# One expert ahead in the feed-forward stage: software pipelining of the two matmul phases on eight cores

## The reference

```python
probs = softmax(xf @ router_w + router_b)          # 64 experts
tw, ti = top_k(probs, 8); tw = tw / sum(tw)
...
def body(acc, p):                                  # p: one of 64 experts, hidden width 256
    W1, B1, W2, B2, e = p
    h = silu(xf @ W1 + B1) @ W2 + B2
    cw = sum(where(ti == e, tw, 0.0), axis=-1)
    return acc + cw[:, None] * h
...
shared = sum over 2 experts, hidden width 2048, of silu(xf @ SW1 + SB1) @ SW2 + SB2
```

## Time and profile before

| | |
|---|---|
| median of 2 runs | 8694.64 us (8684.18 to 8705.1) |
| the profiled execution | 8689.07 us |
| its span on the slowest core (core 5) | 8687.5 us |
| spans of cores 0 to 3 | 8566.1 to 8582.3 us |
| spans of cores 4 to 7 | 8629.4 to 8687.5 us |
| feed-forward stage from its first routed unit | about 4150 to 8500 us |

### The profile page before, as it was taken

The page is one execution under the profiler, slowest core; times in us unless marked ns, Lnnn a source line. Parts: engine busy times, 40 slices in busy tenths (PEclk is TensorE's granted clock), DMA queues, the critical chain, the costliest instruction groups (busy, mean ns, idle before and its releaser), DMA issues.

```text
span 8687.5 us, 72076 instructions; the slowest of 8 cores (8566.1 to 8687.5 us)
## 1 busy us (share of the span) xinstructions
PE 5028.5 (58%) x21600; PEld 2213.4 (25%) x21600; DVE 2143.5 (25%) x4862; ACT 1571.8 (18%) x3527; POOL 246.9 (3%) x300
## 2 busy tenths in 40 slices
PE   3554544645454545421666666666666667668881
PEld 1221221222222222210222222222222222223440
DVE  2333333331323222234111111111111111111113
ACT  1222222121212121222111111111111111111112
POOL 0000000001010000000000000000000000000000
PEclk8666666767575756655788887888888887777885
DMA  2000000005030312110211111111111001111202
GB/s 49 10 20 10 10 20 10 10 10 70 8 45 11 40 19 34 22 31 19 37 20 20 20 20 20 20 20 20 20 20 20 9 11 20 20 20 20 39 1 75
DMA packets 265490, 200.20 MB, mean 23 GB/s; under 512 B 142020, under 2 KB 224068, under 8 KB 265110
## 3 DMA queue, kind: packets, MB, share of 16 engines
q0 software_dynamic: 244448, 128.23, 11.4%
q1 hardware_dynamic: 20662, 67.36, 2.2%
HBM read 307.00 MB, written 16.78 MB: 37 GB/s over the span
## 4 chain that ended last, share of the span: by engine, by line
PE 54%; DVE 16%; ACT 13%; issue 11%; DMA 4%; DVEq 1%; ACTq 1%; another core or an unknown queue 1%; POOL 0%; POOLq 0%; SPq 0%
PE pb L158 54%; DVE h_sc L1046 3%; ACT h_sb L1039 2%; DVE S_state L555 2%; ACT cwb_sb L1021 2%; DVE st_sq L365 2%; DVE st_s L359 2%; DMA wog_buf<-Wog 2%; DVE khb L536 1%; ACT khT L547 1%; ACT xln_fm L406 1%; DVEq L80 1%; DVE st_s L1049 1%; DMA wk_buf<-Wk 1%; ACT Sbf L750 1%
## 5 line engine op out<-in xcount | busy, mean ns | idle before, releaser
L158 PE MATMUL pb<-w2g,h_sc 128*128 128x512 bf16 x5120 | 1678.9, 495 | 881.2 <-DVE st_s L1049 797.2
L158 PE MATMUL pb<-x1ln_fm,w1g 128*128 128x384 bf16 (+1 forms) x7680 | 1339.6, 336 | 283.7 <-ACT cwb_sb L1021 283.7
L158 PEld LDWEIGHTS pb<-w2g,h_sc 128*128 128x128 bf16 x5120 | 575.9, 118 | 1862.6 <-issue 1723.2
L158 PEld LDWEIGHTS pb<-x1ln_fm,w1g 128*128 128x128 bf16 x7680 | 745.9, 107 | 831.6 <-issue 442.4
L1046 DVE TENSOR_TENSOR h_sc<-h_sb,cwb_sb 128x384 bf16<-128x384 bf16 (+1 forms) x768 | 257.9, 336 | 2812.8 <-ACT h_sb L1039 2770.1
L1076 DVE TENSOR_TENSOR acc<-acc,pb 128x512 f32<-128x512 f32 x640 | 439.8, 687 | 736.5 <-PE pb L158 685.2
L1039 ACT ACTIVATE h_sb<-pb,b1T_sb 128x384 bf16<-128x384 f32 (+1 forms) x768 | 419.2, 546 | 955.4 <-PE pb L158 953.8
L1021 ACT CAST cwb_sb<-pb 128x384 bf16<-128x384 f32 (+1 forms) x384 | 170.3, 444 | 2201.5 <-PE pb L158 2201.5
L158 PE MATMUL pb<-Wv_sb,xln_fm 128*128 128x512 bf16 x2048 | 445.1, 379 | 0.0
L158 PE MATMUL pb<-v_tm,khT 128*128 128x256 bf16 x512 | 189.8, 371 | 288.8 <-ACT khT L547 216.9
L158 PE MATMUL pb<-iI128b,khb 128*128 128x128 bf16 x512 | 141.9, 277 | 335.7 <-DVE khb L536 335.7
(11 more groups left out here) (146 smaller groups left out, 3805.0 us busy)
## 6 DMA issues: line engine op xcount, KB each, us to landing
w1g<-w POOLq DMA_DIRECT2D x64, 512.0 KB, 14.1
w2g<-w POOLq DMA_DIRECT2D x64, 512.0 KB, 15.7
x_tm<-x_pre SPq DMA_DIRECT2D x12, 2048.0 KB, 9.2
wog_buf<-Wog POOLq DMA_DIRECT2D x64, 256.0 KB, 4.6
x_tm<-x_own SPq DMA_DIRECT2D x4, 2048.0 KB, 7.6
wq_buf<-Wq POOLq DMA_DIRECT2D x32, 256.0 KB, 5.1
wk_buf<-Wk POOLq DMA_DIRECT2D x32, 256.0 KB, 5.2
x_sp<-x_tm SPq DMA_DIRECT2D x16, 512.0 KB, 2.6
```

Source lines behind the costliest of these rows:

```text
L158: fn = lambda E, o=out, l=lhsT, r=rhs, st=start, sp=stop: E.matmul(o, l, r, start=st, stop=sp)
```

## The change

The loop body over the four units of a tile is cut in two functions. `front` holds everything up to the product with `cwb_sb`, `back` the 12 (or 4) matmuls with `w2g`. `back` of a unit is now emitted after `front` of the next one, and the last `back` of a tile after the one before it. `cwb_sb` and `h_sc` get two places, used in turn (`par`); `h_sb` is gone, the `Silu` writes `h_sc` and the product is formed in place. All three matmul groups of a front go into one bank, `pb[6 + par]`. The copy on `st_s1` is gone; TensorE waits for the product itself. The first ScalarE write of a front waits for the product of the front two before (`scale_tok`).

```diff
-                for j, (kind, e) in enumerate(grp):
+                def front(j, kind, e):
+                    par = j % 2
+                    bankh = pb[6 + par]
                     b.wait("t", wtoks[slot])
                     if kind == "r":
-                        bank6 = pb[6]
                         b.wait("t", tk_cwT)
-                        mm(b, bank6, bank6.sl(0, tscnt),
+                        mm(b, bankh, bankh.sl(0, tscnt),
                            selg[:, j * 128:(j + 1) * 128],
                            cwT64[:, ts0:ts0 + tscnt], start=True, stop=True, seal=True)
...
+                        b.wait("s", scale_tok[par])
+                        pbread(b, bankh, "s",
+                               lambda E, bankh=bankh, par=par, tscnt=tscnt: E.copy(
+                                   cwb_sb[:, par, 0:tscnt], bankh.sl(0, tscnt)))
+                    else:
+                        b.wait("s", scale_tok[par])
                     for hc in range(2):
-                        bankh = pb[6 + hc]
                         for kc in range(8):
                             mm(b, bankh, bankh.sl(0, tscnt),
...
-                            dst = h_sb
...
+                        dst = h_sc
...
                     if kind == "r":
                         b.wait("v", tk_h)
                         for hc in range(2):
...
+                                h_sc[:, par, hc, 0:tscnt], h_sc[:, par, hc, 0:tscnt],
+                                cwb_sb[:, par, 0:tscnt], ALU.mult))
-                        tk_hsc = b.opi("v", lambda E: E.tensor_copy(
-                            st_s1[:, 0:1], st_s1[:, 0:1]))
-                        b.wait("t", tk_hsc)
+                        scale_tok[par] = b.tok("v")
                     else:
-                        b.wait("t", tk_h)
+                        scale_tok[par] = tk_h
+                    return scale_tok[par]
+
+                def back(j, kind, e, rdy):
+                    par = j % 2
+                    b.wait("t", rdy)
                     for tq in range(ntq):
...
+                pend = None
+                for j, (kind, e) in enumerate(grp):
+                    rdy = front(j, kind, e)
+                    if pend is not None:
+                        back(*pend)
+                    pend = (j, kind, e, rdy)
+                back(*pend)
```

More of the change, by code:

```diff
@@ L824, in emit_ffn @@
         selm = fsb("selm", [64, 1], F32)
-        cwb_sb = fsb("cwb_sb", [128, 384], BF16)
-        h_sb = fsb("h_sb", [128, 2, 384], BF16)
-        h_sc = fsb("h_sc", [128, 2, 384], BF16)
+        cwb_sb = fsb("cwb_sb", [128, 2, 384], BF16)
+        h_sc = fsb("h_sc", [128, 2, 2, 384], BF16)
+        scale_tok = [None, None]
         x1a = fsb("x1a", [128, D], F32)
@@ L1011, in emit_ffn @@
                     b.wait("t", tk_sel)
-                for j, (kind, e) in enumerate(grp):
+                def front(j, kind, e):
+                    par = j % 2
+                    bankh = pb[6 + par]
                     b.wait("t", wtoks[slot])
                     if kind == "r":
-                        bank6 = pb[6]
                         b.wait("t", tk_cwT)
-                        mm(b, bank6, bank6.sl(0, tscnt),
+                        mm(b, bankh, bankh.sl(0, tscnt),
                            selg[:, j * 128:(j + 1) * 128],
                            cwT64[:, ts0:ts0 + tscnt], start=True, stop=True, seal=True)
-                        pbread(b, bank6, "s",
-                               lambda E, bank6=bank6, tscnt=tscnt: E.copy(
-                                   cwb_sb[:, 0:tscnt], bank6.sl(0, tscnt)))
+                        b.wait("s", scale_tok[par])
[4 more added lines that the diff above has]
+                        b.wait("s", scale_tok[par])
                     for hc in range(2):
-                        bankh = pb[6 + hc]
                         for kc in range(8):
@@ L1035, in emit_ffn @@
                             bias_ap = sb1T_sb[:, ci_ * 2 + hc, si:si + 1]
-                            dst = h_sc
+                        dst = h_sc
                         pbread(b, bankh, "s",
-                               lambda E, bankh=bankh, hc=hc, bias_ap=bias_ap,
+                               lambda E, bankh=bankh, par=par, hc=hc, bias_ap=bias_ap,
                                dst=dst, tscnt=tscnt: E.activation(
-                                   dst[:, hc, 0:tscnt], bankh.sl(0, tscnt),
+                                   dst[:, par, hc, 0:tscnt], bankh.sl(0, tscnt),
                                    AF.Silu, bias=bias_ap, scale=1.0))
@@ L1045, in emit_ffn @@
                         for hc in range(2):
-                            b.op("v", lambda E, hc=hc, tscnt=tscnt: E.tensor_tensor(
-                                h_sc[:, hc, 0:tscnt], h_sb[:, hc, 0:tscnt],
-                                cwb_sb[:, 0:tscnt], ALU.mult))
-                        tk_hsc = b.opi("v", lambda E: E.tensor_copy(
-                            st_s1[:, 0:1], st_s1[:, 0:1]))
-                        b.wait("t", tk_hsc)
-                    else:
-                        b.wait("t", tk_h)
[L1054 to L1060, removed]
+                            b.op("v", lambda E, par=par, hc=hc, tscnt=tscnt: E.tensor_tensor(
+                                h_sc[:, par, hc, 0:tscnt], h_sc[:, par, hc, 0:tscnt],
+                                cwb_sb[:, par, 0:tscnt], ALU.mult))
+                        scale_tok[par] = b.tok("v")
+                    else:
+                        scale_tok[par] = tk_h
[3 more added lines that the diff above has]
+                    b.wait("t", rdy)
                     for tq in range(ntq):
@@ L1067, in emit_ffn @@
                                 mm(b, bank, bank.sl(0, 512),
-                                   h_sc[:, hc, tq * 128:(tq + 1) * 128],
+                                   h_sc[:, par, hc, tq * 128:(tq + 1) * 128],
                                    w2g[slot][:, j * 2 + hc, half * 512:(half + 1) * 512],
                                    start=first_w, stop=last, seal=last)
+                pend = None
[5 more added lines that the diff above has]
+                back(*pend)
                 for tq in range(ntq):
```

## The result

The changed kernel's median is 7855.46 us over 12 runs (7723.72 to 8004.66); the kernel before, run beside it, has 8725.97 us over 10 runs. The ratio of the two is 0.8889, 95% interval 0.8828 to 0.8949: faster by 11%. The forecast was 7890 us. Those are 8566 to 8582 us before (cores 0 to 3) and 7715 to 7736 us after (cores 0 to 3), 850 us apart.

The account below looks back on a forecast made before the run. The prediction took matmuls and short hand-overs to DVE and ACT, not memory, to bound the kernel. From 8689 us, stalls 452 and clock 391 less, the die's slow stretch 38 more: 7884, said as 7890 us; range 7740 to 8250.

Parts of the forecast that it names:

- The overlap's stalls: Routed units: the 2.13 us hole goes, one of 0.88 us is added; 400 + 63 - 11 = 452 us less.
- The bank's hole: Between a unit's halves: half 1 waits until Silu has read half 0, 0.88 us full and 0.67 us small.
- the cast's hole stays as it is: Routed units: TensorE's wait for the cast was to remain 0.77 us, with no cost counted.
- The clock: Routed groups: without the long hole full tiles stay at 2.4 GHz; 442 - 107 + 56 = 391 us less.
- The start of a group: Behind building selg: matmuls run at 1.2 GHz until a back runs; 6.7 us x 16 = 107 us lost.
- The small tile: Small routed units: staying warm would give 113 us; half was taken, 56 us gained.
- the copy itself: The copy on st_s1, the in-place product and the two places of cwb_sb were said to cost nothing.
- The die's slow stretch: Late routed groups on core 5: about two groups at a reduced clock, 38 us lost.
- The shared groups: Shared groups: time unchanged, the wait for Silu only moves to between the halves, 0.88 for 0.88 us.
- A: Rival: in the routed groups the clock alternates as before and only the stalls are gained; 8240 us, chance 0.12.
- C: Rival: clock falls at a group's start, doesn't rise again, needing a stretch without holes; some 9470 us, chance 0.02.
- B: Rival: one die, or both, held at 0.8 of the clock for the whole routed part; 8210 us, chance 0.11.

Follow-up runs that it names:

- e4: The kernel before without the copy on st_s1, TensorE waiting for the second product instead; 8063 to 8076 us on cores 0 to 3.
- d2: The changed kernel with the copy on st_s1 put back behind the products; 7731 to 7739 us on cores 4 to 7.
- e1: The changed kernel without the overlap, each back right behind its own front; 8548 to 8601 us on cores 4 to 7.
- e8: The kernel before with the weight row's matmul and cast ahead of the previous unit's second layer, three units of four; 7999 to 8019 us, cores 4 to 7.
- d1: The kernel before with two copies on st_s1 in a row; 8649 to 8676 us, ratio 1.0037 to the kernel before.
- e5: The changed kernel with a bank per half, weight row one unit early, units running on over tiles and groups, selg built ahead; 6728 to 6760 us, ratio 0.7800.

## Why the prediction was right, point by point

**The overlap's stalls.** Right. The 2.13 us hole went to nothing inside the full tiles, the new one is 0.88 us, the unit 7.43 us as forecast. PE's idle time ahead of the two layers fell from 881.2 + 283.7 to 726.7 + 8.6 us, 430 less, against 452. The bank's hole, which no routed row had shown, came as sized. What was missed is in the row of 1.18 us: at a tile's start two fronts follow each other, and the second one's cast queues on ACT behind the first one's last Silu. The timeline shows it:

```profile
5946.42 0.58 ACT L1041 ACTIVATE h_sc<-pb,b1T_sb 128x384 bf16<-128x384 f32 x1 [1.76 <-PE pb L158]
5947.09 0.48 ACT L1023 CAST cwb_sb<-pb 128x384 bf16<-128x384 f32 x1
```

That is 319.0 - 283.7 = 35 us, a term that I costed at nothing ("the cast's hole stays as it is"). The small tile's end gave 0.53 us each, where 0.7 stood.

**The clock.** Right in size, and only half right in its reason. The forecast gave 391 us; of the 850 us between the cores 0 to 3 of before and after some 420 are not stalls. The full tiles run at 2.4 GHz, from its second group to its last core 0 takes 176 us a group against the 178 forecast, and the mean granted clock of the stretch is 0.95 on core 1 (0.93 on core 0 with the first group). The start of a group costs 18.6 us against 12.7 for the same matmuls later, 6 us, where I had 6.7, and that only in 9 of 15 groups: 64 us for the 15 together, where I had 107 for 16. The small tile was put at half warm; on core 0 93 of its 128 runs of 8 first-layer matmuls are at 2.4 GHz. But I had laid the falls to the one long hole and credited the clock to the overlap, and that is too much: by e4 removing the copy alone, which leaves 1.87 us, restores it as well (411 us), and by d2 the overlap alone does. The weak step is "the copy itself [...] cost nothing", as a statement on the old order; in the changed kernel it holds (d2). That the number came out needed no more than that either of the two sufficed.

**The die's slow stretch.** Right as a kind. The slowest core was 8687 - 8575, about 110 us, behind cores 0 to 3 before, and 7850 - 7722, about 130 us, after: 20 us more, where I had counted 38. But it isn't the die that is held. In both kernels it is two cores of it at a time. Shared groups before, cores 4 and 6, and after, cores 4 and 7:

```profile
7850.00:8400.00 550.00, 468.22 (x2154) 225.31 (x2193) 74.20 (x108) 90.06 (x164) 18.91 (x24) 0.81 0.15 24
...
7850.00:8400.00 550.00, 454.57 (x2474) 230.47 (x2475) 89.75 (x146) 103.20 (x192) 19.26 (x24) 0.98 0.15 24
```

```profile
7060.00:7620.00 560.00, 467.18 (x2565) 238.03 (x2608) 94.06 (x148) 110.03 (x204) 19.24 (x24) 1.00 0.16 23
...
7060.00:7620.00 560.00, 488.29 (x2265) 230.13 (x2263) 78.35 (x114) 93.10 (x169) 12.82 (x16) 0.82 0.12 20
```

Core 5 goes with core 4, and 6 with 7. In the changed kernel cores 4 and 5 had their turn from 5800 to 6600 us (0.81 and 0.80, with 6 and 7 at 0.95 and 0.94). So the prediction's remark that core 5's 0.80 agrees with a rule on the whole die doesn't hold: cores 6 and 7 of the same die had full clock in the same groups.

**The shared groups.** Right: a full unit is 6.23 us at full clock before and after, the wait only changed its place.

**The rivals.** A (clock alternates) and C (it never rises) did not happen: behind the first unit of all no hole over 1.2 us is left in a tile of core 0, and the rise came in the first back of a group at the latest. C's premise, that a rise needs a stretch without holes, does not hold in the same timeline: in 5 of the 15 groups it came between the two halves of the first front, at 4903.52 us for one, with a hole of 0.77 us ahead of the first half and of 0.88 us ahead of the second. B happened on two cores at a time, for part of the stage. The Trainium skill's section that I weighed for A (TensorE: Matmul & The Clock Gate, "A second HAM failure mode: psum-queue depth-cycling") has the pauses between groups of matmuls make the clock go up and down. The kernel before agrees with it, at 0.83 with pauses of 0.77 and 2.13 us; e1, which pauses more often (0.77, 0.88 and 1.87 us in a unit), does not, at 0.92.

## What to carry to other kernels

- Where TensorE's clock alternates, a few tenths of a us on a chain that it waits for can be worth several times themselves: look for the hole ahead of the matmuls that run at half speed, and shorten that one first, by whatever instruction is the cheapest to drop (e4). Taking another hole out of the unit helps the clock too, though less (e8).
- An overlap pays what it takes away less what its new buffers make wait. Give the banks to what is read late, half by half, and not to the unit: the change as made took 850 us off, with one bank a half it takes off some 1400.
- Count again at the seams (first and last unit of a tile, first of a group): that is where the order changes for the other engines too.

## What the runs showed of the hardware

- A quarter of a microsecond decided over the clock. Beside a 0.77 us hole per unit, one of 1.87 us left it up (mean 0.93), 2.13 and 2.39 us had it alternate (0.83 both), in units that are otherwise the same.
- Length alone is not the whole rule. Behind the same 2.13 us 65 of some 290 full backs of the kernel before kept 2.4 GHz. And 1.87 us of idle time, harmless in e4, were followed by a fall in 85 of 196 backs of e8 (core 5, mean 0.89), where a short matmul stands ahead of the hole and no other hole in the unit. What decides stays open; that it has to do with when in time the hole falls, d1's rival, was not tested apart.
- On its way up the clock passed over holes of 0.77 and 0.88 us, in 5 of 15 groups of the changed kernel.
- Eight cores with TensorE 97 to 99% busy for 1600 us kept 1.00 in the profiled execution of e5, while in the profiled executions of the kernel before and of the changed one two cores at a time, 4 and 5 or 6 and 7, were held at about 0.81 for part of the stage with TensorE far less busy, and the other two of the die weren't at the time. What sets that off was not found.
